# Experts stage with attention: where GpSimd computes the lower attended half, and how far behind SyncE turns the attended rows

## The reference, cut to what matters

```
# experts: every token is sent to its 2 best of 16 experts
a = silu(llinear(x, W1, b1)[1:]);  s = a * llinear(x, W3, b3)[1:]
h = concat(sqrt(sum(s*s) + 1), s)          # the first element is a "time", a root
out = llinear(h, W2, b2)                   # again with a root as its first element
# linear attention, kernel elu(x)+1, 16 heads of 16
z = 1 / (einsum(q, k.sum) + 1e-6)
attended = einsum(q, kv, z)                # later multiplied by w_out
```

## Time and profile before

| | us |
|---|---|
| median of three runs | 2031.93 (2031.28 to 2034.19) |
| the profiled execution's own time | 2035.27 |
| its span | 2033.5 |
| first and last attended transposition issued by SP | 403.8 and 924.1 |
| mean granted TensorE clock | 0.856 |
| busy: PE, DVE, ACT, POOL | 1402.9, 1363.0, 1219.8, 1213.2 |

### The profile page before, as it was taken

How to read it: one execution, slowest core, us unless ns; L and a number is a source line. 1 busy time by engine, 2 the same in 40 slices (tenths; PEclk the granted TensorE clock), 3 DMA queues, 4 the chain that set the end, 5 groups by cost and what they waited for, 6 DMA issues and landing times. The chain is left out here.

```text
span 2033.5 us, 63622 instructions
## 1 busy us (share of the span) xinstructions
PE 1402.9 (69%) x21833; PEld 995.6 (49%) x21834; DVE 1363.0 (67%) x3576; ACT 1219.8 (60%) x3356; POOL 1213.2 (60%) x1312
## 2 busy tenths in 40 slices
PE   3479999655555555544233428999999779999947
PEld 3335555544444444432122315666666556666636
DVE  7878887633333333332666649999999568888848
ACT  8548888533333333322556657888886457777746
POOL 6668887211111111114888638999997567777747
PEclk9999999877777777777567769999999989999959
DMA  8547778534344444445566635666665412222228
GB/s 254 170 137 209 209 208 200 114 91 93 91 93 93 93 93 93 93 109 169 155 204 192 186 103 109 123 133 124 126 127 112 84 40 52 52 53 53 54 69 280
DMA packets 495355, 256.26 MB, mean 126 GB/s; under 512 B 359357, under 2 KB 484864, under 8 KB 494720
## 3 DMA queue, kind: packets, MB, share of 16 engines
q1 hardware_dynamic: 482658, 219.11, 44.2%
q0 software_dynamic: 12576, 35.67, 5.5%
HBM read 79.52 MB, written 73.44 MB: 75 GB/s over the span
## 5 line engine op out<-in xcount | busy, mean ns | idle before, releaser
L1513 POOL TENSOR_TENSOR all_late<-experts_se,all_mhalf 128x4 f32<-128x4 f32 (+1 forms) x77 | 76.3, 991 | 465.9 <-DVE experts_se L1703 460.2
L241 PE MATMUL ps<-all_late,l_xq_T 128*128 128x352 f16 x1536 | 252.6, 316 | 61.1 <-DMA l_xq_T<-l_apart 34.6
L241 PE MATMUL ps<-moe_E,experts_hT 128*128 x432 | 92.9, 342 | 251.2 <-DMA experts_hT<-experts_hs 251.0
L241 PEld LDWEIGHTS ps<-all_late,l_xq_T 128*128 (+1 forms) x1536 | 146.9, 99 | 153.1 <-DVE ffn_h L739 45.8
L241 PE MATMUL ps<-l0moe_W,all_xT_all 128*128 128x16 f16 (+2 forms) x1152 | 189.5, 311 | 30.1 <-ACT all_xT_all L940 22.3
L1636 ACT ACTIVATE all_late<-ps 128x510 f32<-128x510 f32 x72 | 42.6, 592 | 277.2 <-PE ps L1564 273.7
L1708 DVE TENSOR_SCALAR experts_se<-experts_so 128x2 f32<-128x2 f32 x72 | 12.2, 169 | 268.5 <-ACT l0moe_W L1638 268.5
L241 PEld LDWEIGHTS ps<-moe_E,experts_hT 128*128 128x128 f16 x432 | 47.0, 117 | 273.6 <-issue 261.8
L241 PE MATMUL ps<-l_Wq,all_xT_all 128*128 128x256 f16 x384 | 75.2, 356 | 151.8 <-DVE both_y L1973 145.6
L2339 POOL TENSOR_TENSOR all_late<-ret_pm,all_late 128x512 f16<-128x512 f32 x128 | 145.4, 1157 | 19.4 <-ACT all_late L2245 19.4
L241 PEld LDWEIGHTS ps<-l0moe_W,all_xT_all 128*128 128x128 f16 x1152 | 83.7, 100 | 112.3 <-ACT all_xT_all L940 26.0
(11 more groups left out here) (300 smaller groups left out, 4643.5 us busy)
## 6 DMA issues: line engine op xcount, KB each, us to landing
rows_dram<-all_late SPq DMA_DIRECT2D x72, 256.0 KB
ret_v<-ret_vpad SPq DMA_DIRECT2D x256, 64.0 KB, 2.0
front_xin<-x SPq DMA_DIRECT2D x16, 512.0 KB, 4.6
x_dram<-front_x SPq DMA_DIRECT2D x16, 512.0 KB, 5.4
all_late<-x_dram SPq DMA_DIRECT2D x64, 128.0 KB
z_dram<-all_late SPq DMA_DIRECT2D x64, 128.0 KB
both_zin<-z_dram SPq DMA_DIRECT2D x16, 512.0 KB, 4.3
both_xin<-x SPq DMA_DIRECT2D x16, 512.0 KB, 4.6
```

The source lines that it names most:

```text
L241: mm = pe.matmul(out, lhs[a], rhs[b], start=first and n == 0, stop=last and n == 2, skip_group_check=True)
L1513: pool.tensor_tensor(rows[:, n % 4, which, :, 0], se[:, u, which], power[:, which], ALU.pow).then_inc(s_time, 1)
```

## The change

GpSimd's `attended_lo` is placed ahead of `times` and six steps behind instead of after it and eight behind; SyncE's `turn_attended` is fourteen steps behind instead of ten. Nothing else differs, and the same instructions are executed.

```diff
-            unrolled(count, [(7, turn_hidden), (0, turn_rows), (11, store), (10, turn_attended)])
+            unrolled(count, [(7, turn_hidden), (0, turn_rows), (11, store), (14, turn_attended)])
...
             for n in range(count + OLAG):
+                if n % 2 == 0 and 0 <= n - 6 < TILES:
+                    attended_lo((n - 6) // 2)
                 times(n)
-                if n % 2 == 0 and 0 <= n - 8 < TILES:
-                    attended_lo((n - 8) // 2)
```

## The result

The changed kernel took 1771.18 us (median of four runs, 1766.56 to 1773.77) against 2032.26 us before on the same chip: a ratio of 0.8712, 95% interval 0.8691 to 0.8732. The forecast was 1758 us, with a range of 1724 to 1800. The profiled execution took 1772.6 us.

The account below looks back on a forecast made before the run. SP's wait for attended_lo bound each pair (16.87 us); afterwards the o16 slot loop would, at T = 8.3. Saving 256.0 us over 30 pairs plus 18 in the tail, 274 from 2035.3, gave 1761 profiled, median 1758; range 1724 to 1800.

Parts of the forecast that it names:

- The loop of before: Once per pair, SP waits for attended_lo and issues turn_hidden late, so PE, ACT, DVE and POOL follow late; about 17 us.
- The slot of o16: attended_hi(p) needs pair p-2's attended transposition landed; this closes a loop over two pairs, 16.65 us, the deciding term.
- The held root: On POOL, attended_lo ahead of the root waits for attended_hi, adding about 1.1 us to ACT's pair; by itself binds nothing.
- The size of T: T is the new time of a pair in the 30-pair stage: forecast 8.3 us, bounds 8.1 to 8.8.
- SP's 1.0 us of slack: SP's spare time per pair in the loop through o16, taken as idle time, not path.
- The tail: From the last attended_hi to the end of SP's last store: 36.1 us before, forecast 18, so 18 saved.
- The first held root: POOL's root held by attended_lo at the stage's start, charged once at 1.1 us.
- SP's queue as the bound: Rival: SP's DMA issue, not the o16 slot, ends last; T = 7.3, 30 us less, 1728; chance 0.20.
- the forecast's floor: SP issues one pair's six DMAs without a pause in 7.30 us, so T is at least 7.3.
- PE's lower clock: Rival, with backed-up DMA: PE's clock still falls or landings double; T 9.5 to 10.3, 1794 to 1818; chance 0.17.
- The shared port: No charge for attended_lo beside DVE's operations; rival: it and hidden_lo exclude each other, T = 8.9, 17 us more; chance 0.04.

Follow-up runs that it names:

- the fastest version: Changed kernel with SyncE's turn_attended twelve steps behind instead of fourteen and attended_lo after the root, six behind: 1741.24 us, ratio 0.8554 to the kernel before.

## Why the prediction was right, and where it was off

- **The loop of before** and its 17 us per pair: right. Either half of the change opens it by itself, which the forecast didn't say. SyncE four steps later meets an `attended_lo` long done; GpSimd two steps earlier has it nearly done when SyncE comes.
- **The slot of o16** as the new bound: right, and shown from four sides. Issued a pair earlier the wait goes (1746.6), first in its step it goes (1747.3), a pair later the loop closes in one pair (14.94 us against 8.05), and ACT's wait for the landing is in the trace.
- **The held root**: the forecast said that by itself it binds nothing and counted it in the loop. Both hold. Without it a pair is 0.62 us shorter (1771.2 against 1752.5), of which up to 0.12 can be `hidden_lo`.
- **The size of T** is the step that was off: 8.69 instead of 8.3, 11.7 us over 30 pairs. Of the 0.4 us, 0.1 is the landing (3.8 us median where 3.6 was taken, half per pair). Up to 0.12 is `hidden_lo` held in 9 cases by 7.1 us in all. What is left, about 0.2, is as much as the run with SyncE's half alone lies above its sum, and that one has no held `hidden_lo`. PE's pauses and SP being busy when `hidden_lo` is done (0.69 us in the turn shown) are in it; they weren't told apart. The forecast wrote off SP's 1.0 us of slack as idle time: that is wrong where the work comes unevenly.
- **The tail**: 20.0 us against 18. **The first held root**: the stage started 1.3 us better than taken (400.76 against 402.1). 11.7 + 2.0 - 1.3 = 12.4 of the 11.6 us by which the profiled execution was above the forecast for it, 1761; the later stages give back the rest.
- **SP's queue as the bound**: not in the changed kernel. In the fastest version SP issues its six DMAs of a pair in 7.6 us (561.49 to 569.11) with hardly a wait, against the 7.30 of the forecast's floor, and most of the pairs take 7.3 to 7.5 us: there it is nearly the bound. DMA is used 0.94 of the time in that stretch (450 to 630 us), and the first hidden transposition of the pair takes 1.35 us to issue instead of the 1.23 of the earlier trace rows; whether SP's queue or the DMA behind it is what ends last was not tested.
- **PE's lower clock**: the granted clock was 0.96 in the stage, and in the fastest version 1.00 (450 to 630 us). The pieces of the turn above that hold PE's work are as long as forecast (2.38 and 3.54 us), so it isn't what T was over by.
- **The shared port**: "at T = 8.3 `attended_lo` falls beside these operations again" was wrong in 9 pairs of the changed kernel, and wrong in nearly every pair once the slot didn't delay `attended_hi`. As a rival it was right in kind, `hidden_lo` blocked until `attended_lo` is done, but its 17 us stood for every pair; the 9 held here add up to 7.1 us.

## What to carry to other kernels

When a wait in an in-order DMA queue is taken away by issuing that transfer later, ask what its landing frees: with two slots, two steps later can turn "hidden" into a loop over two rounds, and two more into a loop over one. Count the whole ring, with what stands ahead in the queue, for every distance, and take one at which neither the queue nor the slot binds: here twelve, with ten (GpSimd ahead) inside its interval. Look at the pairs one by one too: of the 11 us that the longer loop of PE cost, 9 were in one pair. An instruction placed ahead of one on the critical chain costs its own length and its wait, even on an engine that is mostly idle.

## What was not expected of the hardware

- A VectorE instruction of 0.42 us with two inputs in SBUF takes 0.79 to 1.38 us when it starts inside GpSimd's 1.16 us subtraction, and ends about 0.28 us after it. It works both ways. At 595.10 us in the changed kernel `hidden_lo` starts 0.01 us ahead: it takes its usual 0.41 us, and `attended_lo` takes 1.42. GpSimd's root, else 1.01 us, takes 1.19 us where it starts beside a held `hidden_lo` (526.95 above, beside one from 526.27 to 527.27); beside one that isn't held and has run for 0.3 us, it keeps its 1.01.
- The attended transposition lands in 3.3 us after an idle queue and in 3.8 us (median; up to 5.2) in the changed kernel, with DMA in use 0.84 of the time. It isn't the load as such: issued first in SP's step it lands in 3.3 us (median) with DMA in use 0.94. What stands just ahead of it in the queue, the 2 us of rows and a store, is the likelier cause, but no run changes that alone.
- PE pauses 1.5 to 2.5 us once in twelve steps with no releaser, and once 5.3 us at the end of a pass of 24 steps, behind which its granted clock was 0.68 on average over 12 us.
